# Cross-attention and routed feed-forward on one Trainium2 core: the order of work inside the periods of the attention stage

## The reference, cut to what matters

```python
x = x + xattn(layernorm(x), ctx, ctx, mask)     # x: 2 x 1024 x 256, ctx: 2 x 77 x 256
x = x + ffn(layernorm(x))

def xattn(x_q, x_k, x_v, mask):                 # 16 heads of 16
    q, k, v = x_q @ Wq.T + bq, x_k @ Wk.T + bk, x_v @ Wv.T + bv
    scores = einsum('bhqd,bhkd->bhqk', q, k) / sqrt(16)
    attn = softmax(where(mask == 0, -1e9, scores))
    return einsum('bhqk,bhkd->bhqd', attn, v) @ Wo.T + bo

def ffn(xf):                                    # 2048 tokens, 8 experts, 2 each, C = 768
    probs = softmax(xf @ w_router)
    gate, eidx = top_k(probs, 2);  gate /= sum(gate)
    pos = cumsum(one_hot(eidx)) - 1             # place of a token in its expert's list
    keep = pos < C
    expert_in[eidx, pos] += xf * keep
    h = relu(expert_in @ w1 + b1);  y = h @ w2 + b2
    return sum over the two experts of gate * keep * y[eidx, pos]
```

## Time and profile before

| what | us |
|---|---|
| median of three executions | 554.68 (549.78 to 555.1) |
| profiled execution, its own time | 555.85 |
| span of its trace | 554.1 |
| PE busy in the span | 474.3 (86%) |
| DVE, ACT, POOL busy | 284.8, 268.3, 234.0 |
| granted TensorE clock, mean | 0.897 |

### The profile page before, as it was taken

The page is one execution under the profiler, slowest core; times in us unless marked ns, Lnnn a source line. Parts: engine busy times, 40 slices in busy tenths (PEclk is TensorE's granted clock), DMA queues, the critical chain, the costliest instruction groups (busy, mean ns, idle before and its releaser), DMA issues.

```text
span 554.1 us, 10225 instructions
## 1 busy us (share of the span) xinstructions
PE 474.3 (86%) x3757; PEld 444.1 (80%) x3757; DVE 284.8 (51%) x579; ACT 268.3 (48%) x507; POOL 234.0 (42%) x364
## 2 busy tenths in 40 slices
PE   5474989999898978515999999999999999999990
PEld 4353878787777857415999999999999999999990
DVE  3447274788775633211564563745537455465430
ACT  2225254466363541202866765567755577654520
POOL 4612021434744337473043643636436365363531
PEclk9879598999996865655999999999999999999995
DMA  8838289843273101213033341433414334131110
GB/s 259 199 109 265 78 229 279 218 115 123 88 210 115 49 30 48 68 67 117 1 122 101 129 133 39 159 116 141 130 29 165 114 113 147 27 97 38 48 38 1
DMA packets 51767, 63.07 MB, mean 114 GB/s; under 512 B 7515, under 2 KB 46474, under 8 KB 51598
## 3 DMA queue, kind: packets, MB, share of 16 engines
q1 hardware_dynamic: 36118, 41.10, 25.5%
q0 software_dynamic: 6144, 12.64, 6.9%
q10 hardware_dynamic: 9464, 8.79, 5.8%
HBM read 40.97 MB, written 25.72 MB: 120 GB/s over the span
## 4 chain that ended last, share of the span: by engine, by line
PE 59%; POOL 7%; issue 4%; DVE 3%; ACT 1%; DMA 1%; POOLq 0%; DVEq 0%; SPq 0%
PE ps L1161 16%; PE ps L1159 16%; PE ps L1160 16%; POOL expert_in L526 3%; PE ps L1441 2%; PE ps L1260 2%; PE ps L1285 1%; PE ps L1174 1%; PE ps L1304 1%; ACT rows L687 1%; POOL rstd L420 1%; POOL rows L515 1%; DMA xc<-expert_in 1%; DMA expert_in<-rows,sidx 0%; PE ps L1242 0%
## 5 line engine op out<-in xcount | busy, mean ns | idle before, releaser
L792 ACT ACTIVATE hf<-ps,bcol 128x256 f32<-128x256 f32 x192 | 80.0, 468 | 97.1 <-PE ps L1161 97.0
L1159 PE MATMUL ps<-wh,hh 128*128 128x256 f32 x384 | 109.5, 285 | 0.0
L1159 PE MATMUL ps<-xTh,wh 128*128 128x256 f32 x384 | 108.7, 283 | 0.0
L1161 PE MATMUL ps<-xTh,wl 128*128 128x256 f32 x384 | 108.6, 283 | 0.0
L1160 PE MATMUL ps<-xTl,wh 128*128 128x256 f32 x384 | 108.5, 282 | 0.0
L1161 PE MATMUL ps<-wh,hl 128*128 128x256 f32 x384 | 107.7, 280 | 0.0
L1160 PE MATMUL ps<-wl,hh 128*128 128x256 f32 x384 | 107.7, 280 | 0.0
L1110 DVE TENSOR_TENSOR hl<-hf,hh 128x512 fp32r<-128x512 f32 x96 | 66.6, 694 | 78.1 <-ACT hh L798 73.8
L575 POOL DMA_INDIRECT out<-yb,ctok x48 | 51.9, 1082 | 92.8 <-DVE yb L1125 84.3
L567 POOL DMA_INDIRECT acc<-out,ctok x48 | 69.3, 1444 | 37.4 <-issue 22.9
L1159 PEld LDWEIGHTS ps<-xTh,wh 128*128 128x128 f32 x384 | 73.9, 193 | 0.0
(11 more groups left out here) (163 smaller groups left out, 854.7 us busy)
## 6 DMA issues: line engine op xcount, KB each, us to landing
wraw<-in_L_ffn_w SPq DMA_DIRECT2D x16, 1024.0 KB
expert_in<-zrow ACTq DMA_DIRECT2D x6, 1032.0 KB, 7.6
xc<-expert_in SPq DMA_DIRECT2D x24, 258.0 KB
qs<-q_by_head SPq DMA_DIRECT2D x8, 768.0 KB, 5.9
q_by_head<-qh SPq DMA_DIRECT2D x16, 256.0 KB, 2.7
q_by_head<-ql SPq DMA_DIRECT2D x8, 256.0 KB, 3.8
out<-xs SPq DMA_DIRECT2D x4, 512.0 KB
xs<-in_x ACTq DMA_DIRECT2D x1, 1536.0 KB, 11.7
```

What stands on the lines that cost most here:

```text
L792: ins = a.activation(hf[:, i % 2, s * CH:(s + 1) * CH], ps[:, i, s * CH:(s + 1) * CH], ACT.Relu, bias=bcol[:, bass.ds(at(e * MT + 2 * i + ...
L1159: T.matmul(dst, sh, mh, start=first, stop=False)
L1161: return T.matmul(dst, sl, mh, start=False, stop=last)
```

## The change

What moves, engine by engine (nothing of the arithmetic changes; `SPLIT` and `PLAIN` give the same units as before, even and odd):

- POOL: `norm1(i + 3)` goes from ahead of `dispatch(n - 1)` to behind it, and `running(n)` goes behind that in every period. The two copies of token number and gate into `rows` leave `dispatch` and become `tag_rows`, first in a period.
- PE: `positions(n - 1)` goes from just ahead of `logits(n)` to just behind `times_v(w, 0)`, early in the period. `scores(m, 0)` now waits for `slot_ready` of macro m - 4 (count m - 3) from m = 4 on.
- DVE: `slot_values(n - 1)` and `picked(n - 1)` leave the end of the period and go behind `sum_o(w, 0)` and behind `divide_o(w, 0)`. `rest_q(f)` goes ahead of `maximum(i + 1, 0)`, and `rest_p(i, 2)` ahead of `maximum(i + 1, 3)`.
- The front: q of macro 0 is projected ahead of K; the V projection, the turning of Wo and q of macro 2 (with its stores and load on SP) go into period 0, and so do the copies and splits that belong to them on ACT and DVE. SP's own queue keeps its order.

```diff
@@ POOL @@
+            def tag_rows(n):
+
+                pool.wait_ge(S["gates_ready"], n + 1)
+                if n >= 2:
+                    pool.wait_ge(S["scattered%d" % (n % 2)], n // 2 * (2 * G * 16))
+                g.tensor_copy(rows[:, n % 2, :, :, TOK], tokid[:, toks(n), :])
+                g.tensor_copy(rows[:, n % 2, :, :, GATE], gt[:, n % 2])
+
...
             for i in range(NM + 2):
                 n = i - 2
+                if n >= 1:
+                    tag_rows(n - 1)
                 if n >= 0:
                     norm2(n)
-                if i + 3 < NM:
-                    norm1(i + 3)
-                if n >= 0 and i < NM:
-                    running(n)
                 if n >= 1:
                     picks(n - 1)
                 if n == 1:
                     pool.wait_ge(S["zero_done"], 16 * (SLOTS // P // 8))
                 if n >= 1:
                     dispatch(n - 1)
-                if n >= 0 and i >= NM:
+                if i + 3 < NM:
+                    norm1(i + 3)
+                if n >= 0:
                     running(n)
+            tag_rows(NM - 1)
             picks(NM - 1)
             dispatch(NM - 1)
...
@@ ACT @@
-            act.wait_ge(S["wo_turned"], 1)
-            a.activation(woT[:].rearrange("p k d -> p (k d)"), ps[:, 5, :], ACT.Copy).then_inc(S["wo_copied"], 1)
-            copy_xT(2)
-            head_q(2)
-            act.wait_ge(S["vf_ready"], 1)
-            a.activation(vpart(0), vview(vf[:]), ACT.Copy).then_inc(S["vpart_step"], 1)
             copy_mT(0)
...
-                if 3 <= f < NM:
+                if f < NM:
                     head_q(f)
...
@@ DVE, before the loop @@
             normal1(0)
+            stats1(1)
+            dve.wait_ge(S["mask_loaded"], 16)
+            v.tensor_scalar(mb[:, :, 0:NK], mraw[:], 0.0, NEG, ALU.is_equal, ALU.mult).then_inc(S["mask_step"], 1)
+            rest_q(0)
+            normal1(1)
             dve.wait_ge(S["k_projected"], 1)
             dve.wait_ge(S["bias_copied"], 1)
...
@@ DVE, the loop @@
-                if slots and i >= NM:
-                    slot_values(n - 1)
                 if slots:
                     residual(n)
                     stats2(n)
                 if units:
                     rest_p(i, 0)
+                if i == 0:
+                    values()
                 if tail:
                     sum_o(w, 0)
-                if nxt:
-                    maximum(i + 1, 0)
+                if n >= 1:
+                    slot_values(n - 1)
                 if front:
                     rest_q(f)
                 if nxt:
-                    maximum(i + 1, 1)
+                    maximum(i + 1, 0)
                 if tail:
                     divide_o(w, 0)
+                if n >= 1:
+                    picked(n - 1)
+                if nxt:
+                    maximum(i + 1, 1)
                 if units:
                     rest_p(i, 1)
                 if i == 0:
-                    v_rest(1)
-                if slots and i >= NM:
-                    picked(n - 1)
+                    v_rest(0)
                 if nxt:
                     maximum(i + 1, 2)
                 if tail:
                     sum_o(w, 1)
+                if units:
+                    rest_p(i, 2)
                 if nxt:
                     maximum(i + 1, 3)
                     split_max(i + 1)
                 if tail:
                     divide_o(w, 1)
-                if units:
-                    rest_p(i, 2)
+                if i == 0:
+                    v_rest(1)
...
                 if slots:
                     route(n)
-                    if n >= 1 and i < NM:
-                        slot_values(n - 1)
-                if slots:
-                    if n >= 1 and i < NM:
-                        picked(n - 1)
                     gates(n)
@@ PE @@
                     if m >= 4:
                         pe.wait_ge(S["lg_copied"], m - 3)
-                    if m >= 5:
-                        pe.wait_ge(S["slot_ready"], m - 4)
+                        pe.wait_ge(S["slot_ready"], m - 3)
...
+            turn_xn(0)
+            pe.wait_ge(S["wq_copied"], 1)
+            project_q(0)
             pe.wait_ge(S["wk_copied"], 1)
             pe.wait_ge(S["c_summed"], 1)
...
                 if units:
                     scores_t(i, 0)
+                if i == 0:
+                    pe.wait_ge(S["wv_copied"], 1)
+                    for b in range(NB):
+                        for k in range(KT):
+                            ins = T.matmul(ps[0:KV, 4, b * D:(b + 1) * D], cT[:, k, b, :], wvT[:, k, :],
+                                           start=(k == 0), stop=(k == KT - 1))
+                    ins.then_inc(S["v_projected"], 1)
+                    pe.wait_ge(S["wo_loaded"], 16)
+                    turn_weight(3, 5, "wo_turned")
                 if front:
                     turn_xn(f)
...
                 if tail:
                     times_v(w, 0)
+                if n >= 1:
+                    positions(n - 1)
                 if units:
                     scores_t(i, 1)
...
```

More of the change, by code:

```diff
@@ L984, in v_rest, with values @@
                 ins.then_inc(S["vpart_step"], 1)
+            def values():
+                dve.wait_ge(S["v_projected"], 1)
+                dve.wait_ge(S["bv_loaded"], 16)
+                dve.wait_ge(S["const_ready"], 3)
+                for b in range(NB):
+                    ins = v.scalar_tensor_tensor(out=vf[:, b * D:(b + 1) * D], in0=bv_b[:], scalar=bscale[0:KV],
+                                                 in1=ps[0:KV, 4, b * D:(b + 1) * D], op0=ALU.mult, op1=ALU.add)
+                ins.then_inc(S["vf_ready"], 1)
             stats1(0)
@@ L1014, in _ @@
             maximum(0, 1, ST)
-            dve.wait_ge(S["v_projected"], 1)
-            dve.wait_ge(S["bv_loaded"], 16)
-            dve.wait_ge(S["const_ready"], 3)
-            for b in range(NB):
-                ins = v.scalar_tensor_tensor(out=vf[:, b * D:(b + 1) * D], in0=bv_b[:], scalar=bscale[0:KV],
-                                             in1=ps[0:KV, 4, b * D:(b + 1) * D], op0=ALU.mult, op1=ALU.add)
-            ins.then_inc(S["vf_ready"], 1)
             maximum(0, 2, SC)
@@ L1024, in _ @@
             split_max(0)
-            rest_q(2)
-            v_rest(0)
-            dve.wait_ge(S["bo_loaded"], 16)
-            v.tensor_copy(bo_h[:, 0, :], bo3[:]).then_inc(S["bo_step"], 1)
             def rest_bo():
+                dve.wait_ge(S["bo_loaded"], 16)
+                v.tensor_copy(bo_h[:, 0, :], bo3[:]).then_inc(S["bo_step"], 1)
                 dve.wait_ge(S["bo_step"], 1)
@@ L1047, in _ @@
                 f, w, n = i + 2, i - 1, i - 2
-                units, nxt, front, tail, slots = i < NM, i + 1 < NM, 3 <= f < NM, 0 <= w < NM, n >= 0
-                if slots and i >= NM:
-                    slot_values(n - 1)
+                units, nxt, front, tail, slots = i < NM, i + 1 < NM, f < NM, 0 <= w < NM, n >= 0
                 if slots:
@@ L1353, in _ @@
             project_q(1)
-            turn_xn(2)
             pe.wait_ge(S["kst_loaded"], 16 * 4)
             pe.wait_ge(S["mask_copied"], 1)
-            scores(0, 0, SC, 2)
-            scores(0, 1, ST, 2)
-            pe.wait_ge(S["bias_copied"], 1)
-            pe.wait_ge(S["wv_copied"], 1)
-            for b in range(NB):
-                for k in range(KT):
-                    ins = T.matmul(ps[0:KV, 4, b * D:(b + 1) * D], cT[:, k, b, :], wvT[:, k, :],
-                                   start=(k == 0), stop=(k == KT - 1))
-            ins.then_inc(S["v_projected"], 1)
-            scores(0, 2, SC, 2)
-            scores(0, 3, ST, 2)
-            pe.wait_ge(S["wo_loaded"], 16)
-            turn_weight(3, 5, "wo_turned")
+            for p in range(PAIRS):
+                scores(0, p, (SC, ST)[p % 2], 2)
             turn_max(0)
-            project_q(2)
             pe.wait_ge(S["sel_ready"], 4)
@@ L1431, in _ @@
                     project_o(w)
[L1432 to L1433 removed]
+            positions(NM - 1)
             def turn_x(c, par, half):
```

69 lines of the change are left out of this document (30 added, 39 removed).

## The result

The changed kernel takes 589.92 us (median of 4 runs, 589.66 to 591.58); the kernel before took 554.89 beside it (4 runs). The ratio is 1.0661, with a 95% interval of 1.0596 to 1.0726: slower by 35 us. The forecast was 588 with a range of 563 to 607. The profiled execution took 589.66 us, its span is 587.9, its mean granted clock 0.844. Some executions of a kernel, with or without the change, are over 1.5% longer than its fastest; the times given are medians of all of them, the ratios compare only the others, so a ratio is not always that of the two times beside it.

What follows compares the result with a forecast made beforehand. PE was taken as the bound of the attention stage's periods. Front 6.8, new wait 14.4, rest_p 1.4, clock 26, period 6 -5.8, tail -10, tags -0.3 sum to +32.5, giving 588 us, range 563 to 607.

Steps and rivals of the forecast that it cites:

- The new wait: PE idle 3.5 us before the second scores call in periods 0 to 5; periods 1 to 5 cost 14.4 us.
- The clock: PE's clock falls behind each new wait, 5.2 us a period, 26 us over periods 1 to 5.
- the rule that stood beside it: A loop with a PE wait every turn loses its clock every turn, costing half the throttled time: 6.5 us each.
- Periods 1 to 5 together: New wait 12.3 us in periods 1 to 4 and 2.1 in period 5, plus clock 26 and most of 1.4.
- `rest_p`: rest_p(i, 2) ahead of maximum(i + 1, 3) on DVE delays that maximum 0.45 us in six periods: 1.4 us taken.
- The front: Stretch up to period 1: the start of period 1 comes 6.8 us later, bounds 5 to 10.
- Period 6: The 2.31 us PE wait splits into 1.4 and 0.4, and the clock stays up: -5.8 us, other end -0.6.
- The tail: Periods 7 and 8: the 3.19 us wait for rows goes and the clock partly recovers: -10 us, bounds 3.2 to 15.
- clock stays up: Rival: the 3.5 us waits come in periods 0 to 5 but the clock holds; +1.0, 557 us, chance 0.12.
- short falls: Rival: each fall behind the new waits is short, 7.5 us in place of 26; 571 us, chance 0.20.
- long falls: Rival: in four periods the clock is still low when the next starts, about 5 us more each; 608, chance 0.13.
- no gain in the tail: Rival: norm ahead of dispatch gains only 3.2 us or less; 595 us, inside the range, no separate chance.

Runs made afterwards that it cites:

- e2_swap_alone: The kernel before with one edit, rest_q(f) ahead of maximum(i + 1, 0) on DVE: 589.91 us, ratio 1.0708.
- e6_head_early: The changed kernel with ACT's head_q(f) moved ahead of exps(i, 2): 564.57 us, ratio 1.0157 to the kernel before.
- e5_short_filler: The changed kernel with 7 matmuls of unused result put into PE's long waits of periods 1 to 5: 570.47 us, ratio 1.0242 to the kernel before.
- e7_front_and_dispatch: The kernel before with the new front and new dispatch part, DVE's rest_q and rest_p(i, 2) placed as before: 560.18 us, ratio 1.0004.
- e9_norm1_early: e8_bo_wait_late with the first norm of period i + 3 earlier on DVE and POOL: 548.54 us, ratio 0.9817 to the kernel before.
- e4_dispatch_part: The kernel before with only the routing part: second norm ahead of dispatch, tags first, positions, slot_values and picked early: 547.31 us, ratio 0.9912.
- e8_bo_wait_late: e4_dispatch_part with PE's wait for bo moved from period 0's end to ahead of the first output projection: 549.80 us, ratio 0.9864 to the kernel before.

## Why the prediction was right

**The new wait (14.4 us).** Right in place, length and cause. Six waits of 3.51 or 3.52 us, predicted "3.5 us in one piece". e2_swap_alone makes them by two calls that change places, e6_head_early shortens them through ACT as the chain says.

**The clock (26 us).** Right in kind, and somewhat too dear. It fell behind all six waits and stayed at 0.50 for about 13.5 us in periods 1 to 5, and for 27 behind the wait of period 0. e5_short_filler gives the price alone: 23 us, from the difference of two ratios with intervals of 0.0065 and 0.0085, so plus or minus 6, and 17.9 by the traces; a period cost 3.6 to 4.6 and not 5.2. Of the rule that stood beside it (the Trainium skill, "TensorE: Matmul & The Clock Gate", section "HAM oscillation — how this bites in real kernels") the trace agrees in the first half, that every turn of the loop loses its clock; half of the throttled time, 6.5 us a turn, is more than the 3.6 to 4.6 measured.

**Periods 1 to 5 together (12.3 + 2.1 + 26, and most of the 1.4).** +36.4 measured against +41.6. The periods grew by 8.2, 5.9, 8.2, 7.7 and 6.5 us, where 3.07 + 5.2 is 8.3 and period 5 was to grow by 7.3. Half of the difference is period 2, which had some low clock already (0.92 in the earlier trace rows), and a fall can't be paid for twice. But period 1 had too (0.77) and grew by the full 8.2, as the low stretch from period 0 reached into it.

**`rest_p` (1.4, bounds 0 to 2.7).** 3.5 by the ratios with zero inside the interval: not told apart.

**The front (6.8, bounds 5 to 10).** 8.2 us by the start of period 1; 5 (1 to 9) by e7_front_and_dispatch, which has no 3 us wait in period 0. Step by step: first scores 29.85 (said 31), first `scores_t` 37.29 (said 39), second call of scores 50.49 (said 49.4), `bo_h` 64.5 (said 62.4 without the low clock). The added 5 us for a low clock were shared out otherwise: it stood at 0.50 from 26 to 43 us and again from 50 to 77, so a part of that price is paid in period 1.

**Period 6 (-5.8, other end -0.6).** This is the step that failed; the range was wide enough for it. I took the slot wait as 1.4 us, and 1.31 was measured. But I took the clock as staying up, because the nearest row, 1.30 us in period 5, had left it alone. It fell, to 0.50 from 213.7 to 227. So period 6 gained 0.3 and not 5.8. The other end of the bound was the truth.

**The tail (-10, bounds 3.2 to 15).** -9.5. The wait of 3.19 us is gone, period 7 runs at 1.00 to about 250, and from there the clock is at 0.50 as I had guessed for a part of period 8. e9_norm1_early shows how much of it hangs on the clock: the same instructions can take 10 us more. The size was hit partly by luck.

**The sum.** The errors are -5 (periods 1 to 5), +1.4 (front), +5.5 (period 6), +0.5 (tail), about -1 (the stretches behind), and they nearly cancel. That the total came within 2 us of the forecast is therefore luck; that it came inside the range is not, since wait and clock are shown each by itself. The rivals: clock stays up, refuted by mean clocks of 0.60 to 0.76 in periods 1 to 5; short falls, refuted by the stretches of 13.5 us; long falls, seen once, from period 0 into period 1, while the later low stretches ended 3 us or more before the next period; no gain in the tail, refuted by 9.5 us.

## What to carry to other kernels

Before an instruction is moved ahead of another on an in-order engine, follow what it waits for. If that chain leads back to the engine that waits for the other one, the two will take turns, however much slack the busy shares show. Price the idle time on TensorE twice: by its length, and by what the clock takes behind it. The second was the larger here (some 18 to 23 of 36 us in periods 1 to 5). Put a wait where its value is used, and when the loop gets faster, look again at what is queued behind long work on GpSimd.

## What the runs showed that I had not expected

- Waits of nearly one length go both ways. 1.31 us in period 6 of the changed kernel brought the clock down, 1.30 us in period 5 of the kernel before did not the earlier trace rows; in e6_head_early 1.45 us in period 4 did and 1.44 us in period 3 did not. The length of a single wait alone doesn't decide it in these traces, and the falls at 161.5 us of e4_dispatch_part and at 186.5 of e9_norm1_early came with no wait over 0.6 us shortly before.
- The 7 filler matmuls, fp32 with 256 columns, are 14 records and took 3.19 us, 0.46 us each; 13 took 5.78.
- The same tail of 226 matmul records took 29.48 us in one version and 40.13 in another, by the clock alone (0.84 and 0.56).
- POOL's subtraction for `xn`, 128x512, took 1.04 us at 120.49 and 2.84 us at 142.87 in e8_bo_wait_late, where DVE was running the 2.29 us `wl` of 128x2048 from 142.52.
